# Raw keys and a transfer in place of two TensorE transposes in a pipelined delta rule

## The chip, the cores and the metric

The kernel runs on one core of a Trainium2 chip. The metric is device time in microseconds (us) for one execution of the whole program.

## The reference

A decoder layer on x of shape (4, 512, 512): a gated delta rule attention, a retention-like cross attention, and a ternary feed-forward net, each after a layer norm and added to x. The change touches the first alone:

```python
mixed = jax.nn.silu(_causal_conv1d(hidden_states @ w_qkv, conv_w))
q, k, v = jnp.split(mixed, [KDIM, 2 * KDIM], axis=-1)
q = _l2norm(q.reshape(Bb, Ss, HK, DK))          # x * rsqrt(sum(x*x) + eps), per token and head
k = _l2norm(k.reshape(Bb, Ss, HK, DK))
...
def step(St, inp):                               # over 512 tokens, per head
    q_t, k_t, v_t, g_t, b_t = inp
    St = St * jnp.exp(g_t)[..., None, None]
    v_old = jnp.einsum('bhk,bhkv->bhv', k_t, St)
    delta = (v_t - v_old) * b_t[..., None]
    St = St + k_t[..., None] * delta[:, :, None, :]
    return St, jnp.einsum('bhk,bhkv->bhv', q_t, St)
```

There are 16 key heads (HK), 32 value heads (two per key head), and head width 128. The output of each head is RMS-normed, gated with silu(z) and projected.

## The kernel before

`head` makes the normed input (xT, features on partitions) and tables of decays. `delta_rule` does the attention up to the output rows in DRAM (core_rows). `tail` does the rest. The change is inside `delta_rule`.

The work of `delta_rule` is cut into 64 units: 16 key heads times 4 batches (ITERS = 64). A unit holds one key head, its two value heads (GV = 2) and 512 tokens in four chunks of 128 (NC = 4). Within a chunk the step recurrence becomes a triangular system; its inverse is built in six levels. The units are software-pipelined. In slot u, unit n = u is projected (`project`), unit m = u - 1 is inverted (`invert`), unit s = u - 2 is run through the recurrence (`recur`), and unit f = u - 3 is finished (`finish`). TensorE, VectorE, ScalarE, GpSimd and the DMA queue (SyncE) each have a `slot` function in which this order is written out by hand. An engine runs its list in order and waits on semaphores, so a waiting instruction holds up all that stand behind it.

The steps and their lines on TensorE: `tile(n, j)` L722 projects a tile of k, q, v0 or v1 (j = 0, 1, 2, 3), `z_tile` L735 the gate; `turn` L742 is four transposes into a PSUM bank; `products` L747 is the four 128x128 products of `kk` and `kq`. `level_z` is L790 and `level_d` L803, eight small f16 products each, `level_e` L815. `solve` is L864, `read_q` L851, `read_k` L843, `grow` L872 and `attend` L883.

On VectorE: `convolve` L1007 is a tap of the causal convolution, `decays` L1016 a scan, `level_z` L1042, `level_d` L1046, `level_e` L1052, and `flip_d` L1035 the transpose of the inverse inside 32x32 blocks. `next_state` is L1072 and `residual` L1066. `flip_v` L1022 and `flip_o` L1027 turn values and outputs.

A level of the inverse goes back and forth between the two engines: TensorE `level_z(m, l)` waits for d_added of the level before; VectorE masks the result (`level_z`, z_ready); TensorE `level_d(m, l)` waits for z_ready and for `flip_d` of the level before (flipped); VectorE adds it (`level_d`, d_added).

The keys before the change: silu writes `kraw` (features on partitions). `k_turn` turns it into bank 2, so that tokens lie on partitions; ScalarE sums the squares, GpSimd makes the norm factor `rk` (L579, L582), and `normal_k` writes `khat`, the normed keys, token-major. `khat_turn` turns them back, ScalarE copies them to `kT`, and `kk` and `kq` multiply from kT. The queries stay raw; `q_turn` turns them for the sum of squares alone (`q_square`, L1195), which enters the RMS norm of the output.

All projections share three PSUM banks. RING_ORDER and RING_BANK say in which order and where; `ring_free` makes a step wait until the step that last had its bank is read. The waits of the ring for bank 1:

```python
RING_FREED = {... "v1": (taps, "taps", 11), ...}   # the last tap of v1, VectorE convolve(n, 3, 3)
```

Of the kernel before, what the change touches and what calls it, by code (L numbers as in the profile page):

```python
# [37 lines left out]
STORES = 16 * NC * NC  # L38

# [275 lines left out]
def delta_rule(nc, xT, tabs, cons, nw, wc, w_loaded, taps_loaded, acc, early_loaded, early_weighed, decay_dram, w_dram, v_dram, core_dram, wout):  # L315

    with ExitStack() as ctx:
# [22 lines left out]
        kss, qss, rkt, rk = sb("kss", [P, NC]), sb("qss", [P, NC]), sb("rkt", [P, NC]), sb("rk", [P, NC])  # L340
# [10 lines left out]
        tab_ready, decay_loaded, gam_ready, gamc_ready, gams_ready = sem("tab_ready"), sems("decay_loaded"), sem("gam_ready"), sem("gamc_ready"), sem("gams_ready")  # L351
        k_turned, k_squares, rk_ready = sem("k_turned"), sem("k_squares"), sem("rk_ready")
        khat_ready, khat_turned, kT_ready, ks_ready = sem("khat_ready"), sem("khat_turned"), sem("kT_ready"), sem("ks_ready")
        q_turned, q_squares, eq_ready = sem("q_turned"), sem("q_squares"), sem("eq_ready")
# [71 lines left out]
        def per_token(ap):  # L426
# [5 lines left out]
        RING_ORDER = ("q", "k", "z1", "v1", "k_turn", "z0", "kq", "v0", "khat_turn", "q_turn", "kk")  # L432
        RING_BANK = {"q": 1, "k": 2, "z1": 0, "v1": 1, "k_turn": 2, "z0": 0, "kq": 2, "v0": 0, "khat_turn": 2, "q_turn": 2, "kk": 1}
        RING_FREED = {"k": (taps, "taps", 2), "q": (taps, "taps", 5), "v0": (taps, "taps", 8), "v1": (taps, "taps", 11),
                      "z0": (z_silued, "z_silued", 0), "z1": (z_silued, "z_silued", 1),
                      "k_turn": (khat_ready, "squares", NC - 1), "khat_turn": (kT_ready, "once", 0), "q_turn": (q_squares, "squares", NC - 1),
                      "kk": (kk_copied, "once", 0), "kq": (kqs_ready, "once", 0)}
# [9 lines left out]
        RING_LAG = {"q": 1, "k": 0, "z1": 2, "v1": 0, "k_turn": 0, "z0": 2, "kq": 1, "v0": 0, "khat_turn": 0, "q_turn": 1, "kk": 0}  # L447
# [24 lines left out]
        def _(sp):  # L472
# [5 lines left out]
            def load_decay(n):  # L478
                g, b = n[0] * (ROUND // B) + n[1] // B, n[1] % B
                src = decay_dram[g, :, b, :] if isinstance(g, int) else decay_dram[bass.ds(g, 1), :, b, :].rearrange("a h s -> (a h) s")  # L480
                wait(sp, gam_ready, at(back(n, 2), GV, GV))
                sp.dma_start(decay[n[1] % 2][:, :, :], bc(src, P, 0)).then_inc(decay_loaded[n[1] % 2], 16)
# [3 lines left out]
            def slot(n, project, invert, recur, finish):  # L486
                if n[0] * ROUND + n[1] < ITERS - 1:
                    load_decay((n[0], n[1] + 1))
# [6 lines left out]
                if project:  # L495
                    next_weights(n, 3)
                if invert:
# [11 lines left out]
                if project:  # L509
                    next_weights(n, 2)  # L510

# [24 lines left out]
            def store_v(m):  # L536
                sp.wait_ge(v_flipped, count(m))
# [27 lines left out]
        def _(pool):  # L565
# [11 lines left out]
            def k_norm(n):  # L577
# [4 lines left out]
                nc.gpsimd.tensor_tensor(rk[:, :], rkt[:, :], cons[:, C_POW:C_POW + NC], ALU.pow).then_inc(rk_ready, 1)  # L582
# [35 lines left out]
            def b_full(n, h):  # L618
                pool.wait_ge(kk_copied, count(n))
# [4 lines left out]
            def p_full(m, h):  # L624
                pool.wait_ge(kqs_ready, count(m))
# [17 lines left out]
            def o_norm(s):  # L643
                pool.wait_ge(o_squares, at(s, GV * NC, GV * NC))
                nc.gpsimd.tensor_tensor(m2[:, :, :], oss[:, :, :], bc(eq[s[1] % 4][:, :], GV), ALU.add).then_inc(or_ready, 1)
# [17 lines left out]
            def slot(n, project, invert, recur, finish):  # L663
# [32 lines left out]
                if project:  # L696
                    gate_strict(n, 0)
                    b_full(n, 0)
# [5 lines left out]
                if invert:  # L704
                    q_norm(m)
                    decayed_keys(m, 1)

# [3 lines left out]
        def _(pe):  # L711
# [38 lines left out]
            def k_turn(n):  # L750
                pe.wait_ge(silued, nth(n, "silued", 0))
                ring_free(n, "k_turn")
                turn(bank("k_turn"), kraw, k_turned)

            def khat_turn(n):
                pe.wait_ge(khat_ready, at(n, NC, NC))
                ring_free(n, "khat_turn")
                turn(bank("khat_turn"), khat[n[1] % 2], khat_turned)

            def q_turn(n):  # L760
                pe.wait_ge(silued, nth(n, "silued", 1))
                ring_free(n, "q_turn")
                turn(bank("q_turn"), qT[third(n)], q_turned)

            def kk(n):
                pe.wait_ge(kT_ready, count(n))
                ring_free(n, "kk")
                products(bank("kk"), kT[third(n)], kT[third(n)], kk_done)

            def kq(m):  # L770
                pe.wait_ge(kT_ready, count(m))
                pe.wait_ge(silued, nth(m, "silued", 1))
                ring_free(m, "kq")
                products(bank("kq"), kT[third(m)], qT[third(m)], kq_done)
# [66 lines left out]
            def read_k(s, c):  # L841
                state_ready(s, c)
                nc.tensor.matmul(psa[:, 0:GV * P], chunk(kT[third(s)], c), state[:, :], start=True, stop=True).then_inc(ks_s, 1)  # L843
# [53 lines left out]
            def slot(n, project, invert, recur, finish):  # L897
# [82 lines left out]
                if invert:  # L980
                    level_z(m, 3)
                    q_turn(m)
# [3 lines left out]
                if project:  # L986
                    kk(n)
# [9 lines left out]
        def _(dve):  # L997
# [12 lines left out]
            def decays(n, h):  # L1010
# [3 lines left out]
                dve.wait_ge(decay_loaded[r % 2], q * (ROUND * 8) + (r // 2 * 16 + 16))  # L1014
                wait(dve, bf_ready, nth(n, "bf_ready", h, 1))
                nc.vector.tensor_tensor_scan(gam[h][:, :], decay[r % 2][:, h, :], ident[:, :], 0.0, ALU.mult, ALU.add).then_inc(gam_ready, 1)  # L1016

            def flip_v(m):
# [3 lines left out]
                nc.vector.transpose(vb[:, :, :, :], vraw[:, :, :].rearrange("p h (c b j) -> p b (h c) j", c=NC, b=NC)).then_inc(v_flipped, 1)  # L1022

# [57 lines left out]
            def slot(n, project, invert, recur, finish):  # L1081
# [81 lines left out]
                if invert:  # L1163
                    level_e(m, 4)
# [4 lines left out]
        def _(act):  # L1169
# [8 lines left out]
            def silu(n, j):  # L1178
                act.wait_ge(taps, nth(n, "taps", 3 * j + 2))
                if j == 0:  # L1180
                    wait(act, k_turned, count(n, 1))
                if j >= 2:
                    wait(act, v_flipped, count(n, 1))
                v = vraw
                out = (kraw[:, :], qT[third(n)][:, :], v[:, 0, :], v[:, 1, :])[j]
# [7 lines left out]
            def squares(src, spare, dst, sem_, scale=1.0):  # L1193
                for c in range(NC):
                    nc.scalar.activation(junk[:, spare + c, :], chunk(src, c), ACT.Square, scale=scale,  # L1195
                                         accum_out=dst[:, c:c + 1]).then_inc(sem_, 1)

            def k_square(n):
                act.wait_ge(k_turned, count(n))
                wait(act, rk_ready, at(back(n, 1), 2, 1))  # L1200
                wait(act, q_squares, at(back(n, 2), NC, NC))
                squares(bank("k_turn"), 0, kss, k_squares)

            def q_square(n):
                act.wait_ge(q_turned, count(n))
# [921 lines left out]
```

## Time and profile before

| | us |
|---|---|
| median of 3 runs | 3333.22 |
| lowest and highest | 3330.68, 3338.06 |
| the profiled execution | 3335.47 |
| its span | 3333.6 |
| its granted clock of TensorE, mean | 0.991 |

The median and the profiled execution are two different executions; a sum made on the trace is made against 3335.47. `delta_rule` fills about the first 2490 us of the span. A slot repeats there with the same pattern, so that one slot can be read for all. In the rows, L790 and so on are lines of the kernel before. Buffer numbers are left out of names: acc is any of the four PSUM banks of the ring and of td, d_conv either convolution buffer. A row of a timeline that says x8 holds eight instructions and their common duration; the start of the next row of the same engine says when that engine went on.

### The profile page before, as it was taken

What the parts mean: (1) busy time and instruction counts of PE and PEld (TensorE: products, weight loads), DVE (VectorE), ACT (ScalarE), POOL (GpSimd) and SP (SyncE); (2) the same over time, 40 slices, a digit from 0 to 9 for tenths busy, and PEclk for the clock granted to TensorE, in tenths of its full rate; (3) what the DMA queues carried; (4) which work ended last, traced back from release to release, by engine and by line L of the source; (5) the groups of instructions that cost most, each with busy time, mean ns of one, the idle gap of its engine ahead of it and who ended that gap; (6) DMA issues with size and microseconds to landing.
All of it is one profiled execution on the core that took longest, in us unless ns stands there. A gap on an engine that the chain in (4) does not pass through costs nothing. (4 is left out here: it accounts for less than half of the span.)

```text
span 3333.6 us, 59535 instructions
## 1 busy us (share of the span) xinstructions
PE 3238.8 (97%) x20832; PEld 2152.7 (65%) x20832; DVE 2414.8 (72%) x3622; ACT 1541.4 (46%) x4983; POOL 1863.5 (56%) x1824
## 2 busy tenths in 40 slices
PE   5899999999999999999999999999988999999999
PEld 2577777777777777777777777777764444454444
DVE  6799999999999999999999999999940011034453
ACT  2455556555655555556555655565631000011232
POOL 2677777777777777777777777777740000011132
PEclk8999999999999999999999999999989999999999
DMA  2122322323232323322332233223215222211001
GB/s 101 42 61 77 70 71 58 77 64 71 64 77 64 71 65 71 73 65 61 78 71 69 58 78 67 67 66 77 75 52 211 76 101 101 76 38 64 0 13 38
DMA packets 373958, 231.85 MB, mean 70 GB/s; under 512 B 290304, under 2 KB 323200, under 8 KB 368128
## 3 DMA queue, kind: packets, MB, share of 16 engines
q1 hardware_dynamic: 372368, 220.97, 25.4%
q10 hardware_dynamic: 1296, 7.08, 0.5%
q8 instruction: 170, 2.79, 0.4%
q14 instruction: 124, 1.02, 0.1%
HBM read 156.39 MB, written 71.57 MB: 68 GB/s over the span
## 5 line engine op out<-in xcount | busy, mean ns | idle before, releaser
L722 PE MATMUL acc<-xT,wc 128*128 128x512 f32 x2048 | 935.8, 600 | 2.8 <-PEq L111 2.0
L722 PEld LDWEIGHTS acc<-xT,wc 128*128 128x128 f32 x2048 | 370.2, 191 | 373.2 <-issue 372.5
L1007 DVE SCALAR_TENSOR_TENSOR d_conv<-acc,wc,d_conv 128x511 f32<-128x511 f32 (+2 forms) x768 | 567.0, 738 | 42.7 <-ACT d_conv L1176 33.5
L735 PE MATMUL acc<-wc,xT 128*128 128x256 f32 x2048 | 473.4, 384 | 0.0
L735 PEld LDWEIGHTS acc<-wc,xT 128*128 128x128 f32 x2048 | 379.1, 190 | 46.2
L622 POOL TENSOR_TENSOR d_bf<-d_kks,d_gam 128x512 f32<-128x512 f32 x128 | 160.3, 1273 | 317.9 <-ACT d_kks L1222 317.9
L1530 PE MATMUL acc<-t_area 128*128 128x512 f32 x768 | 332.5, 592 | 1.0 <-ACT t_area L1979 1.0
L1035 DVE STREAM_TRANSPOSE d_em<-d_dm 128x1024 f16<-128x1024 f16 x256 | 314.5, 1229 | 2.2
L2036 POOL TENSOR_SCALAR t_veps<-t_mv 128x1 f32<-128x1 f32 x32 | 9.7, 303 | 546.1 <-DVE t_mv L1775 546.1
L1042 DVE TENSOR_TENSOR d_zm<-d_tz,cons 128x512 f16<-128x512 f32 x384 | 259.1, 675 | 52.7 <-PE d_tz L790 47.7
L1765 DVE TENSOR_TENSOR t_x<-acc,t_x 128x512 f32<-128x512 f32 x16 | 11.1, 692 | 392.4 <-PE acc L1530 392.4
L1176 ACT ACTIVATE d_conv<-acc,wc 128x512 f32<-128x512 f32 x256 | 175.0, 683 | 183.2 <-PE acc L722 107.5
L1530 PEld LDWEIGHTS acc<-t_area 128*128 128x128 f32 x768 | 144.6, 190 | 177.4 <-issue 177.1
L656 POOL TENSOR_TENSOR d_oo<-d_oo,d_sz 128x512 f32<-128x512 f32 x128 | 159.9, 1269 | 162.5 <-ACT d_oo L1228 162.5
L1016 DVE TENSOR_TENSOR_SCAN d_gam<-d_decay,d_ident 128x512 f32<-128x512 f32 x128 | 247.2, 1931 | 1.4 <-DMA d_decay<-decay_rows 1.4
L640 POOL TENSOR_TENSOR d_imd<-cons,d_dm 128x512 f16<-128x512 f32 x128 | 211.7, 1654 | 59.9 <-ACT d_dm L1245 59.9
L1046 DVE TENSOR_TENSOR d_dm<-acc,d_dm 128x512 f16<-128x512 f32 x256 | 175.6, 686 | 49.2 <-PE acc L803 49.2
L1927 ACT ACTIVATE xT<-t_turn 128x512 f32<-128x512 f32 x32 | 18.2, 596 | 369.7 <-PE t_turn L1512 369.7
L790 PEld LDWEIGHTS d_tz<-d_dm,d_bh 128*128 128x128 f16 x3072 | 136.9, 98 | 75.2 <-issue 39.5
L803 PEld LDWEIGHTS acc<-d_zm,d_em 128*128 128x128 f16 x3072 | 138.5, 98 | 61.9 <-issue 37.9
L883 PE MATMUL d_psb<-d_uu,d_pT 128*128 128x128 f32 x1024 | 161.2, 280 | 7.1 <-ACT d_oq L1249 7.1
L1258 ACT ACTIVATE d_uu<-d_psa 128x256 f32<-128x256 f32 x256 | 99.6, 389 | 141.0 <-PE d_psa L864 137.8
(227 smaller groups left out, 7084.5 us busy)
## 6 DMA issues: line engine op xcount, KB each, us to landing
d_decay<-decay_rows SPq DMA_DIRECT2D x64, 512.0 KB, 5.2
v_rows<-d_vb SPq DMA_DIRECT2D x256, 128.0 KB, 2.3
d_vn<-v_rows SPq DMA_DIRECT2D x64, 512.0 KB, 3.6
core_rows<-d_ob SPq DMA_DIRECT2D x1024, 32.0 KB, 1.7
t_area<-core_rows SPq DMA_DIRECT2D x30, 1024.0 KB, 4.8
wc<-in_w SPq DMA_DIRECT2D x96, 256.0 KB, 3.3
t_x<-in_x SPq DMA_DIRECT2D x4, 1024.0 KB, 9.6
t_area<-in_wout ACTq DMA_DIRECT2D x2, 2048.0 KB, 13.4
```

Source lines behind the costliest of these rows:

```text
L622: nc.gpsimd.tensor_tensor(bf[h][:, :], kks[:, :], gam[h][:, :], ALU.mult).then_inc(bf_ready, 1)
L640: nc.gpsimd.tensor_tensor(half_of(imd, 5)[:, :, 0, :], bc(cons[:, C_ID + (1 - side) * HALF:C_ID + (2 - side) * HALF], GV * NC), half_of(dm ...
L722: last = nc.tensor.matmul(bank(TILE[j])[:, :], wtile(j, k), xT[:, k, r % B * S:(r % B + 1) * S], start=k == 0, stop=k == KT - 1)
L735: last = nc.tensor.matmul(bank(f"z{j}")[:, i * GV * P:(i + 1) * GV * P].rearrange("p (h n) -> p h n", h=GV), xT[:, k, r % B * S + (2 * j + ...
L883: last = nc.tensor.matmul(chunk(psb, h), chunk(pT[s[1] % 2][h], c), chunk(uu, h), start=True, stop=True)
L1007: nc.vector.scalar_tensor_tensor(c[:, d:S], bank(TILE[j])[:, 0:S - d], tap(j, KS - 1 - d), c[:, d:S], ALU.mult, ALU.add).then_inc(taps, 1)
L1016: nc.vector.tensor_tensor_scan(gam[h][:, :], decay[r % 2][:, h, :], ident[:, :], 0.0, ALU.mult, ALU.add).then_inc(gam_ready, 1)
L1035: nc.vector.transpose(em[m[1] % 2][:, :], dm[:, :]).then_inc(flipped, 1)
L1042: nc.vector.tensor_tensor(even(zm[l], l), packed(tz, l), bc(mask, GV * NC), ALU.mult).then_inc(z_ready, 1)
L1046: nc.vector.tensor_tensor(even(dm, l), packed(td, l), even(dm, l), ALU.add).then_inc(d_added, 1)
L1176: nc.scalar.activation(conv_of(TILE[j])[:, :], bank(TILE[j])[:, :], ACT.Copy, scale=tap(j, KS - 1)).then_inc(tap0, 1)
L1530: return nc.tensor.matmul(acc[t][:, :], core_of(grp, t, q, h), rhs, start=head == 0, stop=head == HV - 1)
```

## The change

Keys stay raw. silu writes straight into `kT` (four buffers now), and `kk`, `kq` and `read_k` use raw keys. The key norm enters as a factor per row: the ScalarE copies of kk and kq go chunk by chunk with scale `rk`, and the factor of the residual is a new table `rt` (`state_scale` on GpSimd). kk needs the norm per column too: rk is stored to DRAM and loaded back to all partitions as `krow` (`store_row`, `load_row`), and GpSimd multiplies (`column_scale`). So `khat_turn` and `copy_kT` go. `q_turn` goes as well: VectorE turns the queries in 32x32 blocks (`flip_q`), 16 transfers move the blocks (`move_q`), and `q_square` reads the result a slot later. `copy_kq` is cut into four scaled pieces in the same way as `copy_kk` below. The two buffers of `decay` become one. On TensorE `kk` is placed elsewhere.

```diff
-        RING_ORDER = ("q", "k", "z1", "v1", "k_turn", "z0", "kq", "v0", "khat_turn", "q_turn", "kk")
+        RING_ORDER = ("q", "k", "z1", "v1", "k_turn", "z0", "kq", "kk", "v0")
...
-                wait(sp, gam_ready, at(back(n, 2), GV, GV))
+                wait(sp, gam_ready, at(back(n, 1), GV, GV))
             def slot(n, project, invert, recur, finish):
+                if invert:
+                    next_weights(back(n, 1), 1)
+                if project:
+                    next_weights(n, 0)
+                if invert:
+                    next_weights(back(n, 1), TILES)
+                if project:
+                    next_weights(n, 3)
                 if n[0] * ROUND + n[1] < ITERS - 1:
                     load_decay((n[0], n[1] + 1))
...
+                if project:
+                    store_row(n)
                 if invert:
                     store_v(back(n, 1))
+                if project:
+                    load_row(n)
...
+                if invert:
+                    move_q(back(n, 1))
...
+            def store_row(n):
+                sp.wait_ge(rk_ready, at(n, 2, 2))
+                sp.dma_start(row_dram[n[1] % 2], rk[n[1] % 4][:, :]).then_inc(row_moved, 16)
+            def load_row(n):
+                sp.wait_ge(row_moved, at(n, 32, 16))
+                wait(sp, kk_ready, count(n, 1))
+                sp.dma_start(krow[:, :], bc(row_dram[n[1] % 2].rearrange("p c -> (p c)"), P, 0)).then_inc(row_moved, 16)
+            def move_q(m):
+                sp.wait_ge(v_flipped, at(m, 2, 2))
+                wait(sp, q_squares, at(back(m, 1), NC, NC))
+                for a in range(NC):
+                    for b in range(NC):
+                        sp.dma_start(qn[b * 32:(b + 1) * 32, a].rearrange("p c j -> p (c j)"),
+                                     qf[a * 32:(a + 1) * 32, b].rearrange("p c j -> p (c j)")).then_inc(q_moved, 16)
...
+            def state_scale(n):
+                pool.wait_ge(tab_ready, count(n))
+                pool.wait_ge(rk_ready, at(n, 2, 2))
+                nc.gpsimd.tensor_tensor(rt[n[1] % 4][:, :].rearrange("p (h c) -> p h c", h=GV),
+                                        tab(n, Q_NEGDEC).rearrange("p (h c) -> p h c", h=GV), bc(rk[n[1] % 4][:, :], GV),
+                                        ALU.mult).then_inc(rt_ready, 1)
+            def column_scale(n):
+                pool.wait_ge(kk_copied, at(n, NC, NC))
+                pool.wait_ge(row_moved, at(n, 32, 32))
+                nc.gpsimd.tensor_tensor(by_chunk(kks), by_chunk(kks), krow[:, :].rearrange("p (i c) -> p c i", c=NC), ALU.mult).then_inc(kk_ready, 1)
                     k_norm(n)
+                    state_scale(n)
...
                     gate_strict(n, 0)
+                    column_scale(n)
                     b_full(n, 0)
...
             def kk(n):
-                pe.wait_ge(kT_ready, count(n))
+                pe.wait_ge(silued, nth(n, "silued", 0))
                 ring_free(n, "kk")
...
                     kq(m)
                     level_z(m, 2)
                 if project:
+                    kk(n)
                     tile(n, 2)
                 if invert:
                     level_d(m, 2)
-                if project:
-                    khat_turn(n)
...
                     level_z(m, 3)
-                    q_turn(m)
                 if recur:
                     grow(s, 1)
-                if project:
-                    kk(n)
                 if invert:
                     level_d(m, 3)
...
+            def flip_q(m):
+                dve.wait_ge(silued, nth(m, "silued", 1))
+                wait(dve, q_moved, at(back(m, 1), MOVED, MOVED))
+                nc.vector.transpose(qf[:, :, :, :], qT[third(m)][:, :].rearrange("p (c b j) -> p b c j", c=NC, b=NC)).then_inc(v_flipped, 1)
...
                 if invert:
+                    flip_q(m)
                     level_e(m, 4)
...
             def copy_kk(n):
+                act.wait_ge(rk_ready, at(n, 2, 2))
-                nc.scalar.activation(kks[:, :], bank("kk")[:, :], ACT.Copy).then_inc(kk_copied, 1)
+                for c in range(NC):
+                    nc.scalar.activation(chunk(kks, c), chunk(bank("kk"), c), ACT.Copy, scale=rk[n[1] % 4][:, c:c + 1]).then_inc(kk_copied, 1)
...
                     copy_kq(m)
+                if project:
+                    copy_kk(n)
                 if recur:
                     first_output(s)
-                if project:
-                    copy_kT(n)
...
-                if invert:
-                    q_square(m)
                 if recur:
+                    q_square(s)
                     solved(s, 2)
```

TensorE in the middle of a slot, before. d_qT,d_kT is `kq`, the L722 row is the tile v0, d_khat is `khat_turn`:

```order
L747 MATMUL acc<-d_qT,d_kT 128x128 x4
L790 MATMUL d_tz<-d_dm,d_bh_0 128x64 x4
L790 MATMUL d_tz<-d_dm,d_bh_1 128x64 x4
L722 MATMUL acc<-xT,wc 128x512 x4
L803 MATMUL acc<-d_zm,d_em 128x64 x8
L742 MATMUL acc<-cons,d_khat 128x128 x4
```

And the end of the same slot, before. d_qT is `q_turn`, d_kT alone is `kk`, the last row is `read_k(s, 2)`:

```order
L742 MATMUL acc<-cons,d_qT 128x128 x4
L872 MATMUL d_psa<-d_uu,d_ks_0 128x128
L872 MATMUL d_psa<-d_uu,d_ks_1 128x128
L747 MATMUL acc<-d_kT 128x128 x4
L803 MATMUL acc<-d_zm,d_em 128x64 x8
L843 MATMUL d_psa<-d_state,d_kT 128x256
```

TensorE of the changed kernel, the first of these places. L789 is `products`, L822 `level_z`, L764 `tile`, L835 `level_d`, L896 `solve`:

```order
L789 MATMUL acc<-d_qT,d_kT 128x128 x4
L822 MATMUL d_tz<-d_dm,d_bh_0 128x64 x4
L822 MATMUL d_tz<-d_dm,d_bh_1 128x64 x4
L789 MATMUL acc<-d_kT 128x128 x4
L764 MATMUL acc<-xT,wc 128x512 x4
L835 MATMUL acc<-d_zm,d_em 128x64 x8
L896 MATMUL d_psa<-d_rr,d_tt_0 128x128
```

`kk` stands ahead of tile v0 and of `level_d(m, 2)` now; both transposes are gone, and between `level_d(m, 2)` and `level_d(m, 3)` only `solve`, `read_q`, `level_z` and `grow` are left.

VectorE at the end of a slot of the changed kernel. L1075 is `level_z(m, 4)`, L1068 `flip_d`, L1035 the three taps of v0, L1085 `level_e`:

```order
L1075 TENSOR_TENSOR d_zm<-d_tz,cons 128x16x32
L1068 STREAM_TRANSPOSE d_em<-d_dm 128x1024
L1035 SCALAR_TENSOR_TENSOR d_conv<-acc,wc,d_conv 128x511
L1035 SCALAR_TENSOR_TENSOR d_conv<-acc,wc,d_conv 128x510
L1035 SCALAR_TENSOR_TENSOR d_conv<-acc,wc,d_conv 128x509
L1055 STREAM_TRANSPOSE d_qf<-d_qT 128x512
L1085 TENSOR_TENSOR d_em<-d_te,d_em 128x16x32
```

The row d_qf<-d_qT is new; before, `level_e` stood right behind the taps. The rest of VectorE's list is as it was.

## Rows read from the trace of the kernel before

**Rows 1.** One slot: length, busy PE, PEld, DVE, ACT, POOL; clock, DMA share, GB/s
```profile
1300.41:1337.22 36.81, 36.81 (x286) 27.14 (x285) 34.09 (x51) 21.77 (x75) 27.21 (x27) 1.00 0.26 56
```

**Rows 2.** Timeline of TensorE, end of a slot: start, duration, engine, line, operation
```profile
1295.59 0.40 PE L803 MATMUL acc<-d_zm,d_em 128*128 128x64 f16 x8
...
1297.41 0.63 PE L742 MATMUL acc<-cons,d_qT 128*128 128x128 f32 x4
1297.88 0.61 PE L872 MATMUL d_psa<-d_uu,d_ks 128*128 128x128 f32 x4
1298.33 1.06 PE L747 MATMUL acc<-d_kT 128*128 128x128 f32 x8
1299.22 0.40 PE L803 MATMUL acc<-d_zm,d_em 128*128 128x64 f16 x8
1299.45 0.68 PE L843 MATMUL d_psa<-d_state,d_kT 128*128 128x256 f32 x2
1299.97 0.61 PE L883 MATMUL d_psb<-d_uu,d_pT 128*128 128x128 f32 x4
1300.41 0.40 PE L790 MATMUL d_tz<-d_dm,d_bh 128*128 128x64 f16 x8
```

**Rows 3.** Timeline of VectorE, same stretch; in brackets its idle time and who ended it
```profile
1296.03 0.69 DVE L1046 TENSOR_TENSOR d_dm<-acc,d_dm 128x512 f16<-128x512 f32 x1 [0.18 <-PE acc L803]
1296.75 1.25 DVE L1035 STREAM_TRANSPOSE d_em<-d_dm 128x1024 f16<-128x1024 f16 x1
1297.92 0.65 DVE L1042 TENSOR_TENSOR d_zm<-d_tz,cons 128x512 f16<-128x512 f32 x1
1298.53 0.61 DVE L1072 SCALAR_TENSOR_TENSOR d_state<-d_state,d_tabm,d_psa 128x128 f32<-128x128 f32 x2
1299.65 0.69 DVE L1046 TENSOR_TENSOR d_dm<-acc,d_dm 128x512 f16<-128x512 f32 x1 [0.52 <-PE acc L803]
...
1302.87 2.27 DVE L1007 SCALAR_TENSOR_TENSOR d_conv<-acc,wc,d_conv 128x511 f32<-128x511 f32 x3
1305.71 0.69 DVE L1052 TENSOR_TENSOR d_em<-d_te,d_em 128x512 f16<-128x512 f32 x1 [0.57 <-PE d_te L815]
```

**Rows 4.** Timeline of all engines around `level_z(m, 2)`, one slot later
```profile
1328.10 0.74 DVE L1007 SCALAR_TENSOR_TENSOR d_conv<-acc,wc,d_conv 128x509 f32<-128x509 f32 x1
...
1328.66 0.40 PE L790 MATMUL d_tz<-d_dm,d_bh 128*128 128x64 f16 x8
```

**Rows 5.** Timeline near the end of the delta rule, where TensorE waits for VectorE
```profile
2458.72 0.68 DVE L1062 TENSOR_TENSOR d_tt<-d_te,d_em 128x512 f32<-128x512 f32 x1
...
2459.46 0.38 PE L864 MATMUL d_psa<-d_vn,d_tt 128*128 128x128 f32 x1 [0.22 <-DVE d_tt L1062]
```

**Rows 6.** Groups by line and shape, 1000 to 2000 us: busy us, mean ns | idle
```profile
L1022 DVE STREAM_TRANSPOSE d_vb<-d_vraw 128x1024 f32<-128x1024 f32 x27 | 33.3, 1234 | 0.0
L1235 ACT ACTIVATE d_khat<-acc,d_rk 128x128 f32<-128x128 f32 x108 | 30.8, 368 | 8.4 <-issue 8.4
```

**Rows 7.** Timeline of GpSimd: the norm factor rk, and the first product with kks
```profile
1300.09 2.51 POOL L622 TENSOR_TENSOR d_bf<-d_kks,d_gam 128x512 f32<-128x512 f32 x2 [4.79 <-ACT d_kks L1222]
...
1322.93 1.01 POOL L582 TENSOR_TENSOR d_rk<-d_rkt,cons 128x4 f32<-128x4 f32 x1
...
1330.85 1.27 POOL L593 TENSOR_TENSOR d_gam<-d_gamc,cons 128x512 f32<-128x512 f32 x1
```

**Rows 8.** DMA issues of the page: KB each, median us from issue to landing
```profile
v_rows<-d_vb SPq DMA_DIRECT2D x256, 128.0 KB, 2.3
...
wc<-in_w SPq DMA_DIRECT2D x96, 256.0 KB, 3.3
```

**Rows 9.** Timeline of the DMA queue: issue of one unit's 16 output stores
```profile
1295.38 9.51 SPq L555 DMA_DIRECT2D core_rows<-d_ob  x16
```

**Rows 10.** Busy time in two stretches with TensorE waits (columns as in Rows 1)
```profile
2436.99:2446.08 9.09, 6.58 (x45) 5.68 (x45) 5.72 (x10) 2.53 (x12) 2.60 (x4) 0.62 0.51 141
2446.00:2460.00 14.00, 11.13 (x117) 9.20 (x115) 8.57 (x17) 5.33 (x20) 8.77 (x6) 1.00 0.06 10
```

More of the change, by code:

```diff
@@ L446, in delta_rule @@
                     "zr_ready": (1, 2), "closed": (2, 1), "tt_ready": (2, 1)}
-        RING_LAG = {"q": 1, "k": 0, "z1": 2, "v1": 0, "k_turn": 0, "z0": 2, "kq": 1, "v0": 0, "khat_turn": 0, "q_turn": 1, "kk": 0}
+        RING_LAG = {"q": 1, "k": 0, "z1": 2, "v1": 0, "k_turn": 0, "z0": 2, "kq": 1, "v0": 0, "kk": 0}
         CONV_LAG = {"k": 0, "v1": 0, "v0": 0, "q": 0}
@@ L752, in k_turn @@
                 ring_free(n, "k_turn")
[L753 to L763, printed above, removed]
+                turn(bank("k_turn"), kT[n[1] % 4], k_turned)
             def kk(n):
-                pe.wait_ge(kT_ready, count(n))
+                pe.wait_ge(silued, nth(n, "silued", 0))
                 ring_free(n, "kk")
-                products(bank("kk"), kT[third(n)], kT[third(n)], kk_done)
+                products(bank("kk"), kT[n[1] % 4], kT[n[1] % 4], kk_done)
             def kq(m):
-                pe.wait_ge(kT_ready, count(m))
+                pe.wait_ge(silued, nth(m, "silued", 0))
                 pe.wait_ge(silued, nth(m, "silued", 1))
                 ring_free(m, "kq")
-                products(bank("kq"), kT[third(m)], qT[third(m)], kq_done)
+                products(bank("kq"), kT[m[1] % 4], qT[third(m)], kq_done)
             def piece(t, h, c):
@@ L842, in read_k @@
                 state_ready(s, c)
-                nc.tensor.matmul(psa[:, 0:GV * P], chunk(kT[third(s)], c), state[:, :], start=True, stop=True).then_inc(ks_s, 1)
+                nc.tensor.matmul(psa[:, 0:GV * P], chunk(kT[s[1] % 4], c), state[:, :], start=True, stop=True).then_inc(ks_s, 1)
             def read_q(s, c):
@@ L1180, in silu @@
                 if j == 0:
-                    wait(act, k_turned, count(n, 1))
+                    wait(act, ks_s, at(back(n, 4), 3, 3))
                 if j >= 2:
-                    wait(act, v_flipped, count(n, 1))
+                    wait(act, v_flipped, at(back(n, 1), 2, 1))
                 v = vraw
-                out = (kraw[:, :], qT[third(n)][:, :], v[:, 0, :], v[:, 1, :])[j]
+                out = (kT[n[1] % 4][:, :], qT[third(n)][:, :], v[:, 0, :], v[:, 1, :])[j]
                 nc.scalar.activation(out, conv_of(TILE[j])[:, :], ACT.Silu).then_inc(silued, 1)
@@ L1200, in k_square @@
                 wait(act, rk_ready, at(back(n, 1), 2, 1))
-                wait(act, q_squares, at(back(n, 2), NC, NC))
-                squares(bank("k_turn"), 0, kss, k_squares)
+                wait(act, k_squares, at(back(n, 1), NC, NC))
+                squares(lambda c: chunk(bank("k_turn"), c), lambda c: junk[:, c, :], kss, k_squares)
             def q_square(n):
-                act.wait_ge(q_turned, count(n))
+                act.wait_ge(q_moved, at(n, MOVED, MOVED))
                 wait(act, eq_ready, count(n, 1))
-                wait(act, k_squares, min(at(back(n, -1), NC, NC), NC * ITERS))
-                squares(bank("q_turn"), 0, qss, q_squares, scale=(RMS_EPS * HD) ** 0.5)
-            def copy_kT(n):
-                act.wait_ge(khat_turned, count(n))
-                nc.scalar.activation(kT[third(n)][:, :], bank("khat_turn")[:, :], ACT.Copy).then_inc(kT_ready, 1)
+                squares(lambda c: qn[:, :, c, :], lambda c: qn[:, :, c, :], qss, q_squares, scale=(RMS_EPS * HD) ** 0.5)
             def b_high(n, h):
@@ L1234, in normal_k @@
                 for c in range(NC):
[L1235 removed]
+                    nc.scalar.activation(chunk(khat[n[1] % 2], c), chunk(bank("k_turn"), c), ACT.Copy, scale=rk[n[1] % 4][:, c:c + 1]).then_inc(khat_ready, 1)
             def copy_kq(m):
@@ L1239, in copy_kq @@
                 wait(act, p_ready, at(back(m, 1), GV, GV))
-                nc.scalar.activation(kqs[:, :], bank("kq")[:, :], ACT.Copy).then_inc(kqs_ready, 1)
+                for c in range(NC):
+                    nc.scalar.activation(chunk(kqs, c), chunk(bank("kq"), c), ACT.Copy, scale=rk[m[1] % 4][:, c:c + 1]).then_inc(kqs_ready, 1)
             def copy_d(m, l, n):
```

60 lines of the change are left out of this document (32 added, 28 removed).

## The prediction

> **What bounds the kernel now.** I read the windows first. In one whole slot, from one `level_z(m, 4)` of TensorE to the next, TensorE is busy 36.81 of 36.81 us, VectorE 34.09, GpSimd 27.21, ScalarE 21.77, and the clock is granted in full, 1.00 [rows 1]. A busy TensorE proves little, since ends of matmuls are modelled, so I went to its timeline: each step starts where the one before it lets it, and no row has a wait in brackets [rows 2]. VectorE's rows do have such brackets: it waits 0.18, 0.52 and 0.57 us for TensorE [rows 3]. So TensorE sets the slot, and VectorE is 36.81 - 34.09 = 2.72 us from doing so. The question is not only how much TensorE loses in work, but whether VectorE can hand back each level of the inverse in time once TensorE comes sooner. I look at the end of the slot, where the edits lie.
>
> **What TensorE saves.** `q_turn` runs from 1297.41 to the start of `grow` at 1297.88, 0.47 us [rows 2]. `khat_turn` is four transposes of the same shape and gets the same 0.47. Together 0.94 us per slot. `kk` is not removed but moved, with 1299.22 - 1298.33 = 0.89 us [rows 2]. Slots with projection and recurrence together are u = 2 to 63, 62 of them. If nothing waited, the gain would be 62 x 0.94 = 58 us.
>
> **What stands in its way.** Before, the stretch from `level_d(m, 2)` at 1295.59 to `level_z(m, 4)` at 1300.41 takes 4.82 us on TensorE [rows 2], and all of it is work. Both turns and `kk` lie in it. All three leave it, so TensorE has 4.82 - 0.94 - 0.89 = 2.99 us of work left there. The chain through VectorE is longer. Let t be the start of `level_d(m, 2)` on TensorE (1295.59 before). From rows 3:
> VectorE `level_d` starts at t + 0.44 (1296.03), `flip_d` at t + 1.16, `level_z(m, 3)` at t + 2.33 and ends 0.65 later at t + 2.98; the two `next_state` start at t + 2.94 and end 0.61 later at t + 3.55.
> A TensorE step that really waits for VectorE starts 0.06 us after it ends: the VectorE operation ends at 2458.72 + 0.68 = 2459.40, TensorE starts at 2459.46 [rows 5].
> So TensorE `level_d(m, 3)`, which needs z_ready, starts at t + 3.04. It would have been ready after d2, solve, read_q, level_z and grow, well under t + 2. `read_k(s, 2)` needs the new state: t + 3.55 + 0.06 = t + 3.61. Behind it `attend` starts 0.52 later and `level_z(m, 4)` 0.44 after that [rows 2], at t + 4.57. (The other way to it, through VectorE's add of level 3, gives t + 3.55 + 0.69 + 0.06 = t + 4.30, which is earlier.) The stretch shrinks from 4.82 to 4.57, by 0.25 us and not by 1.83, and TensorE idles 4.57 - 2.99 = 1.58 us in it.
>
> **What `kk` costs in its new place.** It stands between `level_z(m, 2)` and tile v0, where TensorE has no slack, so t itself comes 0.89 us later. It needs bank 1 back from v1, whose last tap ends at 1328.10 + 0.74 = 1328.84, so 1328.90 with the handoff. TensorE would get there at 1328.66 + 0.23 (the spacing 1299.22 to 1299.45 of such a group) = 1328.89 [rows 2, 4]. So 0.01 us, nothing.
>
> **Per slot:** + 0.89 + 0.01 - 0.25 = + 0.65 us, a slot of 37.46. Before, `kk` filled time in which VectorE was at work on the chain; now it stands ahead of the chain, and the transposes that go were filling the same time.
>
> **The edits that cost nothing as I read them, and what covers them.**
> `flip_q`, VectorE: 128x512 elements, half of `flip_v`, whose mean is 1.234 us [rows 6]; half is 0.62. It stands between the last tap of v0 and `level_e`. There VectorE waits 0.57 us for TensorE: taps from 1302.87, 2.27 long, then `level_e` at 1305.71 [rows 3]. By the chain above VectorE's `level_z(m, 4)` follows TensorE's no later than before, so the wait absorbs it to 0.05 us. Bounds: 0, and 0.62 us per slot if the cover is gone.
> ScalarE: a copy becomes four pieces of 0.368 mean [rows 6], at most 1.47 each for kk and kq, less `copy_kT`. ScalarE has 15 us free in a slot [rows 1], and kk comes 1335.14 - 1328.90 = 6.2 us earlier than it did (1298.33 + 36.81 = 1335.14), so its copy ends earlier as well. `q_square` reads queries moved a slot before.
> GpSimd: `column_scale` is a 128x512 product like the neighbours of 1.27 us, with a strided operand. It can start once `gate_strict` ends at 1330.85 + 1.27 = 1332.12. Before, GpSimd stood idle 4.79 us for kks and began `b_full` at 1300.09, that is 1336.90 a slot later [rows 7]. Now it begins about 1333.4. `state_scale` works on 128x8 elements, far less than any of these, and GpSimd is free 9.6 us of a slot [rows 1].
> The row: rk is ready at 1322.93 + 1.01 = 1323.94 [rows 7]. SyncE needs 9.51 / 16 = 0.59 us per issue [rows 9]; `store_row` and the four `store_v` take five of them, to 1326.9. `store_row` lands in 2.3 by the nearest row, before that. `load_row` lands 3.3 us after it is issued, as a load of 256 KB does [rows 8], at 1330.2. `column_scale` cannot start before 1332.12, and `b_full` is where it was if the row lands by 1335.6. Between 2 and 5 us of cover.
> SyncE: `move_q` adds 16 issues, 9.5 us, to 9.5 for the stores and some 8 others: about 24 us of a 37 us slot. It is ahead of the next slot's decay load; that load's single buffer is free once `decays(n, 0)` has run in the first half of a slot and is read at the start of the next.
> Filling and draining slots (0, 1, 64 to 66) already have TensorE waiting; I take 0 for them, within 2 us.
>
> **The sum.** 62 x 0.65 = 40 us. The profiled execution took 3335.5 and would take 3375.8. The median of the runs is 2.25 lower, so the same sum gives 3333.2 + 40.3 = 3373.5. I forecast 3374, slower. Bounds of this case: with handoffs of 0 instead of two of 0.06, 0.53 per slot, 3366; with `flip_q` in full on the path, 1.27 per slot, 3412. I stay at the low end because the wait that covers `flip_q` stands in a row.
>
> **Rivals.**
> *The gain arrives in full* (faster). If VectorE's chain were not binding, each slot would lose 0.94 us: 3333 - 58 = 3275. It decides where the stretch from `level_d(m, 2)` to `level_z(m, 4)` can be run in less than 4.82 - 0.89 = 3.93 us. For it: TensorE waits nowhere before, and many brackets of VectorE are waits for TensorE. Against it: rows 3 hold 3.55 us of VectorE work and fixed lag alone, ahead of `read_k`. 12 in 100. Somewhere between the two, at no change, 8 in 100.
> *VectorE becomes the bound.* A slot of 36.81 + 0.62 = 37.43, 3372: nearly my time by another cause. The Trainium skill, page "Perfetto Trace Analysis", section "Identifying the Most-Contended Engine", holds that matmul busy time misleads and that TensorE should be judged by the busy share of its weight loads, the other engines by occupancy. By that rule VectorE is the most contended engine here (34.09 against 27.14 us of weight loads [rows 1]), removed transposes bring nothing, and the added one counts in full, which gives that 3372. Against it: VectorE's own waits name TensorE. What tells it apart is VectorE's idle time, which would go to zero. 5 in 100.
> *The row is late.* Beyond 1335.6 each further us is a us per slot, 62 us in all; with one, 3436. 5 in 100.
> *The clock falls.* Before, a stretch with 2.51 us of TensorE idle in 9.09 ran at a granted 0.62, partly at 1.2 GHz, while one with 2.87 idle in 14.00 kept 1.00 [rows 10]. Mine has 1.58 idle in 37.46, all within 4.57. Such a fall would cost 6.58 x 0.38 = 2.5 us per slot: 3374 + 155 = 3529. 4 in 100. The Trainium skill, page "TensorE: Matmul & The Clock Gate", part 1, says that the gate lets half the pulses through unless TensorE has lately been busy; the first of these two stretches agrees.
>
> **How the numbers follow.** My forecast has 66 in 100. A measurement of this kernel tells about 0.2%, 6.7 us, from no change. Slower takes the forecast, VectorE, the row and the clock: 80. Faster 12, same 8. The range takes in no change at its lower end and the full `flip_q` at its upper, 3328 to 3415; it leaves out the full gain, the clock and most of the late row. The forecast's own range is 3366 to 3412.
>
> **What the profile would show.** Right: a slot of about 37.5 us; TensorE waits of 1.6 us per slot, ended by VectorE's `level_z` ahead of `level_d(m, 3)` and by `next_state` ahead of `read_k(s, 2)`; VectorE waiting about 0.9 us more ahead of `level_d(m, 2)`; `flip_q` where 0.57 us of waiting was; no turns beside `k_turn`. Wrong: no such waits and a slot of 35.9 (the full gain); VectorE without idle time; GpSimd waiting for a DMA ahead of `column_scale`; a granted clock under 1.0. Most likely to break the forecast is a chain through VectorE shorter than I add it up, since 0.65 is a difference of larger numbers.

## The result, and the profile after

The changed kernel takes 3516.39 us (median of 4 runs, 3515.33 to 3518.67), the kernel before 3331.95 beside it: a ratio of 1.055, 95% interval 1.053 to 1.057. The direction was forecast, the size was not: 3374 with a range of 3328 to 3415. The span grew from 3333.6 to 3513.5 us, by 179.9.

The start of `flip_o` on VectorE (the row d_ob<-d_oo) comes once a slot, so its spacing is the length of a slot. I took it for 60 slots of each kernel; every fourth of them begins a new key head.

| mean slot, us | before | after |
|---|---|---|
| 45 slots within a key head | 36.81 | 37.50 |
| 15 slots with a new key head | 37.47 | 47.23 |
| sum of the 60 | 2218.7 | 2396.0 |

Of the 177.3 us in these slots, 45 x 0.69 = 31 lie in the ordinary ones and 15 x 9.76 = 146 in the others. So two things have to be read, and they are in different places.

**An ordinary slot.** The timeline of TensorE of the changed kernel, at the stretch of [rows 2]; L835 is `level_d`, L822 `level_z`, L875 `read_k`, L915 `attend`:

```profile
1300.75 0.40 PE L822 MATMUL d_tz<-d_dm,d_bh 128*128 128x64 f16 x8
1301.08 1.13 PE L789 MATMUL acc<-d_kT 128*128 128x128 f32 x8
1302.05 3.60 PE L764 MATMUL acc<-xT,wc 128*128 128x512 f32 x8
1305.48 0.40 PE L835 MATMUL acc<-d_zm,d_em 128*128 128x64 f16 x8
...
1308.52 0.41 PE L835 MATMUL acc<-d_zm,d_em 128*128 128x64 f16 x8 [0.92 <-DVE d_zm L1075]
1309.03 0.70 PE L875 MATMUL d_psa<-d_state,d_kT 128*128 128x256 f32 x2
1309.56 0.61 PE L915 MATMUL d_psb<-d_uu,d_pT 128*128 128x128 f32 x4
1310.01 0.40 PE L822 MATMUL d_tz<-d_dm,d_bh 128*128 128x64 f16 x8
```

And VectorE in the same stretch; the row d_qf is `flip_q`:

```profile
1305.91 0.69 DVE L1079 TENSOR_TENSOR d_dm<-acc,d_dm 128x512 f16<-128x512 f32 x1 [1.15 <-PE acc L835]
1306.64 1.25 DVE L1068 STREAM_TRANSPOSE d_em<-d_dm 128x1024 f16<-128x1024 f16 x1
1307.81 0.65 DVE L1075 TENSOR_TENSOR d_zm<-d_tz,cons 128x512 f16<-128x512 f32 x1
1308.38 0.58 DVE L1106 SCALAR_TENSOR_TENSOR d_state<-d_state,d_tabm,d_psa 128x128 f32<-128x128 f32 x2
...
1314.57 0.70 DVE L1055 STREAM_TRANSPOSE d_qf<-d_qT 128x512 f32<-128x512 f32 x1
1315.30 0.69 DVE L1085 TENSOR_TENSOR d_em<-d_te,d_em 128x512 f16<-128x512 f32 x1
1315.91 1.22 DVE L1044 TENSOR_TENSOR_SCAN d_gam<-d_decay,d_ident 128x512 f32<-128x512 f32 x1
```

With t = 1305.48, `level_d(m, 3)` starts at t + 3.04 and `level_z(m, 4)` at t + 4.53. TensorE waits for VectorE's `level_z` (L1075) where before it had a turn and `kk` to do. VectorE's wait for `level_d(m, 2)` on TensorE has grown from 0.18 [rows 3] to 1.15, because `kk` now delays that step. `flip_q` is in the place of the old wait of 0.57. The whole ordinary slot, in the columns of [rows 1]:

```profile
1272.51:1310.01 37.50, 36.48 (x279) 26.41 (x277) 34.06 (x52) 22.30 (x80) 28.04 (x29) 1.00 0.36 83
```

**A slot with a new key head.** The next rows of the same timelines, in the slot that follows. TensorE:

```profile
1323.06 0.40 PE L847 MATMUL d_te<-d_em,d_zm 128*128 128x64 f16 x8
1330.35 1.19 PE L915 MATMUL d_psb<-d_uu,d_pT 128*128 128x128 f32 x4 [6.89 <-ACT d_oq L1281]
```

VectorE (the row of 1317.04 holds the last three taps of the old key head), and below it ScalarE, which both of them wait for (L1211 is `first_tap`):

```profile
1317.04 2.29 DVE L1035 SCALAR_TENSOR_TENSOR d_conv<-acc,wc,d_conv 128x511 f32<-128x511 f32 x3
...
1329.14 0.75 DVE L1035 SCALAR_TENSOR_TENSOR d_conv<-acc,wc,d_conv 128x511 f32<-128x511 f32 x1 [8.70 <-ACT d_conv L1211]
```

```profile
1328.42 0.69 ACT L1211 ACTIVATE d_conv<-acc,wc 128x512 f32<-128x512 f32 x1 [11.22 <-DMA wc<-in_w]
1329.01 0.36 ACT L1281 ACTIVATE d_oq<-d_psb,d_tabm 128x128 f32<-128x128 f32 x1
```

The DMA queue (SyncE), a row giving the start of the first issue of its kind and the time that all of them took:

```profile
1304.30 9.07 SPq L581 DMA_DIRECT2D core_rows<-d_ob  x16
1313.41 0.45 SPq L479 DMA_DIRECT2D wc<-in_w  x1
1315.30 10.02 SPq L572 DMA_DIRECT2D d_qn<-d_qf  x16
1325.36 1.06 SPq L479 DMA_DIRECT2D wc<-in_w  x2
```

Read from below: the last two loads are the q weights and the convolution taps of the new key head, in this order. The taps have one buffer, so their load waits for the last tap of the old key head, which ends at 1317.04 + 2.29 = 1319.33. But until 1325.3 the queue is busy with the 16 issues of `move_q`, and the load goes out more than 6 us late. ScalarE stands at the first tap 11.22 us. Behind it in ScalarE's list is `read_q` (L1281), so its result for `attend` is late, and TensorE stands 6.89 us. Before, ScalarE's wait for the taps was there too, but shorter. The waits over 100 to 2500 us of the kernel before, the row for these loads:

```profile
ACT d_conv L1176 <- DMA wc<-in_w: 72.2, 15, 5.3
```

and after, over the same window:

```profile
ACT d_conv L1211 <- DMA wc<-in_w: 174.2, 15, 12.7
```

That is 4.8 us at each new key head before, and 11.6 after. TensorE's waits for `read_q` behind that tap, in the same two answers, before and then after:

```profile
PE d_psb L883 <- ACT d_oq L1249: 7.1, 15, 1.0
```

```profile
PE d_psb L915 <- ACT d_oq L1281: 109.2, 15, 8.3
```

So TensorE already waited 0.5 us at each new key head before the change, and waits 7.3 now. It pays once more behind its wait. In windows of the changed kernel (columns as in [rows 1]), 1323.06 to 1338.09 holds the wait and what follows it, 1330.35 to 1338.09 only what follows it, and 1375.82 to 1385.53 is ordinary work:

```profile
1323.06:1338.09 15.03, 8.14 (x44) 5.32 (x41) 7.23 (x12) 4.70 (x15) 7.19 (x6) 0.77 0.31 59
1330.35:1338.09 7.74, 7.74 (x30) 5.01 (x31) 6.02 (x10) 2.80 (x8) 7.19 (x6) 0.68 0.42 70
1375.82:1385.53 9.71, 9.71 (x99) 8.96 (x97) 8.68 (x13) 8.10 (x34) 5.51 (x8) 1.00 0.47 92
```

The granted clock is 0.77 on the mean of the first and 0.68 on that of the second: `attend` takes 1.19 us where it takes 0.61 at 1309.56. From `attend` to the end of tile v1 TensorE needs 7.74 us. The kernel before has the same steps in one of its ordinary slots:

```profile
1313.70:1319.05 5.35, 5.35 (x37) 3.20 (x34) 5.35 (x9) 2.78 (x8) 4.88 (x5) 1.00 0.01 2
```

TensorE is busy throughout in both windows, so the 2.39 us between them are put down to the clock. This slot is 46.94 us long (its `flip_o` starts at 1303.03, the next at 1349.97), 9.44 more than an ordinary one: 6.89 of waiting and 2.39 of slow clock make 9.28 of it.

### The profile page after: what moved, and what is told of

Read it like the earlier page. It is cut to its first block and busy times, and to the rows that moved or that the text cites. A ratio compares the mean times of both kernels' runs of the same rounds, so it can differ in the third digit from the quotient of the medians.

```text
span 3513.5 us, 60809 instructions
## 1 busy us (share of the span) xinstructions
PE 3251.3 (93%) x20320; PEld 2134.0 (61%) x20320; DVE 2414.0 (69%) x3686; ACT 1577.3 (45%) x5303; POOL 1923.5 (55%) x1952
## 3 DMA queue, kind: packets, MB, share of 16 engines
q8 instruction: 166, 2.72, 0.3%
## 5 line engine op out<-in xcount | busy, mean ns | idle before, releaser
L764 PE MATMUL acc<-xT,wc 128*128 128x512 f32 x2048 | 944.0, 604 | 2.1 <-PEq L112 2.0
L1035 DVE SCALAR_TENSOR_TENSOR d_conv<-acc,wc,d_conv 128x511 f32<-128x511 f32 (+2 forms) x768 | 567.4, 739 | 155.9 <-ACT d_conv L1211 146.6
L764 PEld LDWEIGHTS acc<-xT,wc 128*128 128x128 f32 x2048 | 376.7, 194 | 380.8 <-issue 379.8
L678 POOL TENSOR_TENSOR d_imd<-cons,d_dm 128x512 f16<-128x512 f32 x128 | 160.9, 1257 | 384.1 <-ACT d_dm L1277 384.1
L1211 ACT ACTIVATE d_conv<-acc,wc 128x512 f32<-128x512 f32 x256 | 175.6, 686 | 353.0 <-PE acc L764 178.7
L1068 DVE STREAM_TRANSPOSE d_em<-d_dm 128x1024 f16<-128x1024 f16 x256 | 314.7, 1229 | 2.2
L1075 DVE TENSOR_TENSOR d_zm<-d_tz,cons 128x512 f16<-128x512 f32 x384 | 259.9, 677 | 64.5 <-PE d_tz L822 58.0
L915 PE MATMUL d_psb<-d_uu,d_pT 128*128 128x128 f32 x1024 | 169.0, 290 | 109.2 <-ACT d_oq L1281 109.2
L915 PEld LDWEIGHTS d_psb<-d_uu,d_pT 128*128 128x128 f32 x1024 | 146.2, 200 | 115.7 <-issue 112.3
L835 PEld LDWEIGHTS acc<-d_zm,d_em 128*128 128x128 f16 x3072 | 133.2, 98 | 131.6 <-DVE d_zm L1075 74.6
L835 PE MATMUL acc<-d_zm,d_em 128*128 128x64 f16 x3072 | 154.0, 193 | 63.5 <-DVE d_zm L1075 62.4
L1044 DVE TENSOR_TENSOR_SCAN d_gam<-d_decay,d_ident 128x512 f32<-128x512 f32 x128 | 196.8, 1538 | 1.6 <-DMA d_decay<-decay_rows 1.6
L822 PEld LDWEIGHTS d_tz<-d_dm,d_bh 128*128 128x128 f16 x3072 | 138.1, 98 | 77.4 <-issue 36.7
```

Source lines behind the costliest of these rows:

```text
L678: nc.gpsimd.tensor_tensor(half_of(imd, 5)[:, :, 0, :], bc(cons[:, C_ID + (1 - side) * HALF:C_ID + (2 - side) * HALF], GV * NC), half_of(dm ...
L764: last = nc.tensor.matmul(bank(TILE[j])[:, :], wtile(j, k), xT[:, k, r % B * S:(r % B + 1) * S], start=k == 0, stop=k == KT - 1)
L835: last = nc.tensor.matmul(packed(td, l, (h * NC + c) * HALF, HALF), piece(em[m[1] % 2], h, c), even(zm[l], l, (h * NC + c) * P, P), start= ...
L915: last = nc.tensor.matmul(chunk(psb, h), chunk(pT[s[1] % 2][h], c), chunk(uu, h), start=True, stop=True)
L1035: nc.vector.scalar_tensor_tensor(c[:, d:S], bank(TILE[j])[:, 0:S - d], tap(j, KS - 1 - d), c[:, d:S], ALU.mult, ALU.add).then_inc(taps, 1)
L1044: nc.vector.tensor_tensor_scan(gam[h][:, :], decay[:, h, :], ident[:, :], 0.0, ALU.mult, ALU.add).then_inc(gam_ready, 1)
```

## The experiments

All ratios are against the kernel before, run beside the experiment. Slots are given as mean of the 45 ordinary ones / mean of the 15 with a new key head.

**1. Moves later.** The changed kernel, with the moves behind the loads of weights and taps:

```diff
                 if invert:
                     next_weights(back(n, 1), TILES)
+                if recur:
+                    move_q(back(n, 2))
...
-                if invert:
-                    move_q(back(n, 1))
```

> The changed kernel, with the 16 moves of the queries issued in the next slot, behind the loads of the q and k weights and of the taps instead of ahead of them. Theory A (order on the queue): the 15 slots with a new key head, 47.3 us each in the changed kernel, wait because 10.0 us of issues stand ahead of the tap load; they fall to 37.5 to 38.5, and the kernel takes 3516 - 15 x 9.3 = about 3377 us. Theory B (traffic: the moves themselves slow the other transfers, or the clock falls for the steady idle time): the moves are still there, the long slots stay above 44 us, and the time stays above 3460.

3370.87 us, ratio 1.012 (1.010 to 1.013); slots 37.50 / 37.50. Theory A. The transfers are all still there, so neither their traffic nor the steady idle time of TensorE made the long slots. The result is also near the 3374 of the prediction, in part by luck, as the section on the prediction says.

**2. kk back.** On top of experiment 1 (its place in RING_ORDER and its copy on ScalarE go back with it):

```diff
                 if project:
-                    kk(n)
                     tile(n, 2)
...
                     grow(s, 1)
                     head_start(s, 4)
+                if project:
+                    kk(n)
```

> As the kernel with the moves later, and kk back in its old place, between grow and level_d(m, 3), with its copy where it was. Chain theory: kk then fills time in which TensorE waits for VectorE anyway; a slot falls from 37.50 by 0.94 to 36.56, and the kernel by 62 x 0.94 = 58 us against the moves later, to about 3319. Rival (the place of kk is free, and something else lengthens the slot): no change against the moves later, about 3377. Third way: GpSimd gets kks later by the copy in pieces and by column_scale, and part of the gain goes there, 3325 to 3350.

3361.15 us, ratio 1.009 (1.007 to 1.010); slots 37.33 / 37.32. This fits none of the three numbers that were written down: it gained 0.18 us per slot, not 0.94. The third way named the right engine, but took too little of the gain away. The waits between 1000 and 2000 us have a row that was not there before:

```profile
DVE d_zr L1091 <- POOL d_imd L678: 32.4, 26, 1.5
```

VectorE waits 1.2 us per slot for GpSimd's `i_minus_d`. Experiment 9 takes that up.

**3. Keys alone.** The changed kernel without `flip_q` and `move_q`; the queries are turned on TensorE again:

```diff
                     level_z(m, 3)
+                    q_turn(m)
...
-                    flip_q(m)
-                if invert:
-                    move_q(back(n, 1))
```

> The changed kernel with the queries as before: q_turn on TensorE and q_square in the same slot, no flip_q, no moves. Raw keys, the row transfer and the one decay buffer stay. Theory A: slots with a new key head are normal again, about 37.5 to 38.5; the others stay at 37.50, since q_turn fills idle time (2.99 + 0.47 = 3.46 of work in a chain of 4.57). About 3375 us. Rival (the row transfer or the decay load ahead of others causes the long slots): they stay above 44, time above 3460.

3372.53 us, ratio 1.012 (1.011 to 1.014); slots 37.50 / 37.61. Theory A again. Against experiment 1 TensorE has 0.47 us more to do in the stretch, and the ordinary slot is 37.50 in both: work in that gap is free, so removing it brought nothing.

**4. Queries alone.** The kernel before with `flip_q`, `move_q`, no `q_turn`, and the one decay buffer with its place in the queue; keys as before.

> The kernel before with the query part of the change and the one decay buffer: flip_q, moves, no q_turn; keys as before, with khat_turn and kk in its old place. Theory A: the 15 slots with a new key head take about 47; the others have 4.82 - 0.47 = 4.35 us of TensorE work in the stretch and a chain of 4.57, so 36.56. 3333 - 62 x 0.25 + 15 x 9.5 = about 3460 us. Rival (the row transfer makes the long slots): none are long, about 3318.

3449.36 us, ratio 1.035 (1.034 to 1.037); slots 36.52 / 46.37. The long slots come with the moves, and raw keys and the row transfer are not needed for them. The ordinary slot is 0.29 shorter than before: with `kk` in its old place the chain takes over from 4.82 of work. In this run's own timeline `level_d(m, 2)` starts at 1319.72 and `level_z(m, 4)` at 1324.25, 4.53 later.

**5 and 6. Extra issues on the kernel before.** One decay buffer and the new order of loads, and copies of zeros at the end of the slot, 16 of them in experiment 5, 8 in experiment 6:

```diff
                 if project:
                     next_weights(n, 2)
+                if invert:
+                    extra_moves(back(n, 1))
```

> The kernel before with one decay buffer, the new order of the loads on the queue, and 16 extra copies of 16 KB within SBUF per slot, issued at the end of the slot where the changed kernel moves the queries. They carry zeros that nobody reads. No other part of the change. Theory A (issues ahead of the tap load): each of the 15 slots with a new key head gets about 9 us longer, the others stay at 36.81; 3333 + 15 x 9 = about 3468 us. Rival (the loss needs something of the query path, such as q_square waiting for the moves): no change, about 3325 to 3333.

> The same with 8 extra copies per slot instead of 16. Theory A: the queue is occupied 5.0 us instead of 10.0, and the slots with a new key head get about 4.5 us longer; about 3400 us. Rival (a threshold, or a fall of the clock that comes once the wait is there at all): the loss stays near that of 16 copies, or vanishes.

With 16: 3449.18 us, ratio 1.035 (1.033 to 1.036); slots 36.81 / 45.08. With 8: 3344.70 us, ratio 1.003 (1.002 to 1.004); slots 36.81 / 38.18. Experiment 7, which has neither, has 37.43 for the second number. So 16 issues that do nothing for the computation bring 7.65 us per new key head, most of the loss, where about 9 were expected. The dose was wrong: half the issues cost 0.75 us per new key head and not 4.5, which is nearer to the rival's threshold. The waits for the tap load, 100 to 2500 us, first with 16 and then with 8 (both are the same row of ScalarE as above):

```profile
ACT d_conv L1190 <- DMA wc<-in_w: 155.0, 15, 10.8
```

```profile
ACT d_conv L1190 <- DMA wc<-in_w: 82.6, 15, 6.6
```

10.3 and 5.5 us each, against 4.8 before. The queue shows why. In the kernel before, the two loads (q weights and taps) stand at their own waits, and below them is the VectorE row with the last three taps of the old key head:

```profile
1083.44 5.47 SPq L476 DMA_DIRECT2D wc<-in_w  x2
```

```profile
1086.26 2.28 DVE L1007 SCALAR_TENSOR_TENSOR d_conv<-acc,wc,d_conv 128x511 f32<-128x511 f32 x3
```

The two loads take 5.47 us where the changed kernel needs 1.06: the queue stands 4.4 us, until the old weights and taps have been used, the taps last at 1088.54. The same place with 8 issues and with 16:

```profile
1087.15 4.96 SPq L558 DMA_DIRECT2D d_qn<-d_qf  x8
1092.15 1.13 SPq L478 DMA_DIRECT2D wc<-in_w  x2
```

```profile
1125.57 10.02 SPq L558 DMA_DIRECT2D d_qn<-d_qf  x16
1135.63 1.05 SPq L478 DMA_DIRECT2D wc<-in_w  x2
```

Eight issues fill the time in which the queue stood anyway; with them the old taps are read at 1092.93 and the loads have gone by 1093.28. Sixteen outrun it: the old taps are read at 1131.29 and the loads go by 1136.68.

**7. One decay buffer and the order of the loads alone.**

> The kernel before with one decay buffer and the new order of the loads on the queue alone (weights and taps ahead of the decay row). If the one buffer costs a wait, slots get longer than 36.81. If the new order brings the taps sooner, the 15 slots of 37.4 with a new key head fall towards 36.81: 3333 - 15 x 0.6 = 3324 us.

3331.05 us, ratio 0.9996 (0.999 to 1.0005); slots 36.81 / 37.43. The single buffer is free, and so is the new order. The new order does not shorten the slots with a new key head, which I had thought possible.

**8. Queries alone, moves later.** Experiment 4 with the edit of experiment 1.

> The query part alone (keys as before, kk in its old place), with the moves behind the loads of weights and taps. Slots of 36.52 without long ones: 3333 - 62 x 0.29 - 15 x 0.6 = about 3306 us, faster than both kernels. Rival (the moves collide with something else in their new place when the keys take the old path, such as the value stores): slots above 36.81.

3312.48 us, ratio 0.994 (0.993 to 0.995); slots 36.52 / 37.14. This computes the reference and is faster than both kernels, by 0.6% against the kernel before. The slots with a new key head kept their 0.6 us, so it gained 20 us and not the expected 27.

**9. kk back, without the column factor.** Experiment 2 with `column_scale` on one element per partition; the column factor of the key norms is left out of kk:

```diff
-                nc.gpsimd.tensor_tensor(by_chunk(kks), by_chunk(kks), krow[:, :].rearrange("p (i c) -> p c i", c=NC), ALU.mult).then_inc(kk_ready, 1)
+                nc.gpsimd.tensor_tensor(kks[:, 0:1], kks[:, 0:1], krow[:, 0:1], ALU.mult).then_inc(kk_ready, 1)
```

> The kernel with moves later and kk back (37.32 us per slot), with column_scale cut to one element per partition: the column factor of the keys is left out of kk, its waits stay. Theory: kk back gained 0.18 and not 0.94 us per slot because column_scale, 1.54 us between the copy of kk and b_full on GpSimd, made GpSimd late for i_minus_d, for which VectorE waits 1.2 us per slot. Without it that wait goes, and the slot falls to 36.5 to 36.6: 3361 - 62 x 0.75 = about 3315 us. Rival (the copy of kk in four pieces on ScalarE, or the chain through VectorE itself, holds the slot): no change, or less than 0.3 us per slot, above 3343.

3304.02 us, ratio 0.991 (0.989 to 0.993); slots 36.52 / 36.71. The wait of VectorE for `i_minus_d` is down to 7.4 us in 21 times between 1000 and 2000 us. So `column_scale` is what kept experiment 2 from its gain. In the kernel before, GpSimd stood idle 4.79 us, but ahead of kks [rows 7]; `column_scale` comes behind kks, where experiment 2 shows VectorE waiting for it. Here the factor by columns was hidden only with kk computed early (experiment 1), and kk early costs TensorE 0.89 us.

## Why the prediction was right in one place and wrong in another

**The bound and the chain: right.** The prediction has an ordinary slot of 37.46; it is 37.50. It puts `level_d(m, 3)` at t + 3.04, `read_k` at t + 3.61, `level_z(m, 4)` at t + 4.57; the rows give 3.04, 3.55 and 4.53. Experiment 3 shows that work in the gap is free, experiment 9, with `kk` back and little on GpSimd, is 37.50 - 36.52 = 0.98 us below experiment 1; the prediction has `kk` ahead of the chain at 0.90. `kk` came a little later than foreseen: it starts 0.33 after `level_z(m, 2)`, not 0.24. Of the waits that were foretold on TensorE, the trace brackets 0.92 us ahead of `level_d(m, 3)`; the 1.5 are the chain of 4.53 less 2.99 of work.

**`flip_q`, the row, the single buffer: right as read.** `flip_q` took 0.70 us and not 0.62, inside VectorE's old wait. GpSimd waits 2.0 us in all for the row between 1000 and 2000 us of experiment 1. Experiment 7 puts the buffer at nothing.

**The queue: wrong, and this is the step that failed.** The prediction puts the cost of the 16 issues at nothing. It says of `move_q` that it "adds 16 issues, 9.5 us", that SyncE is busy "about 24 us of a 37 us slot", and that it is "ahead of the next slot's decay load". It stops there. Behind the moves also stand the q weights and the taps of the next key head, with ScalarE waiting for the taps 4.8 us already and with no slack: these slots were 37.47 and not 36.81. The issues made that wait 11.6 us and these slots 47.23. I had a mean slot and a sum of busy time, and a wait that comes once in four slots is in neither. The row of waits that names it (72.2 us in 15 times) was in the trace of before. The experiments show it three ways: move the issues (1 and 8), remove them (3), add empty ones (5), and each time the long slots go or come with them. It cost 146 of 180 us.

**The sum for ordinary slots: 31 us, not 40.** It counted 62 slots at 0.65. The 15 with a new key head were at 37.47 already, and experiment 1 has them at 37.50, so only the other 45 grew. That experiment 1 still lands at 3371 is partly luck: its span is 36.0 us longer than before, 31 of it in the 60 slots and 5.3 ahead of the first `flip_o` (at 189.43, before at 184.10), where the prediction took 0 within 2 us.

**The clock: right to be a rival, wrong in its place.** The steady idle time, 1.5 us per slot, left the clock alone (1.00 in the ordinary slot above; experiment 1: a mean of 0.99, as before). It fell behind waits of 7 us, and added 2.4 us in the slot that was read. The sum of that rival, 3529, comes near the result by accident: it had every slot slow.

**VectorE as the bound: did not happen.** It is idle 37.50 - 34.06 = 3.44 us of an ordinary slot, and was idle 2.72 before. In experiment 4, where TensorE lost 0.47 us of work and `kk` stayed in its place, the slot fell to 36.52.

**What stays open.** The 16 empty issues make slots of 45.08, the real moves of 46.37 and 47.23. Part of the first difference is in the waits for the tap load, 10.3 us with the empty issues and 11.8 in experiment 4: `move_q` itself waits for `flip_q` and starts later. The difference between the last two contains a chain that is also longer; it was not taken apart. The 0.6 us of the old slots with a new key head are for the most part the 0.5 us in which TensorE waits for `read_q`. That row is in experiments 7 and 8 as well (6.4 and 6.5 us in 15 times) and gone in 1 and 2; why the tap comes in time there was not shown.

## What to carry to other kernels

Where work is removed from an engine that never waits, add up the chain through the other engines over the same stretch: the slot cannot become shorter than the chain, and a step moved out of the stretch to a place without idle time is paid in full. When a transfer is added to a queue, list everything that is issued behind it in every kind of slot, also in those that come once in four, and look in the waits for the few that name a DMA: a wait of 5 us that costs almost nothing is a sign that the slack is used up. Several small issues in a row are one long one: here 16 of them take 10 us, with queries and with zeros alike.

## What the runs showed of the hardware

VectorE's scan (two inputs in SBUF) takes 1.22 us when GpSimd is idle as it starts and about 2.0 to 2.1 when GpSimd is at work. In the changed kernel GpSimd waits during one scan of each ordinary slot, and the mean of all scans falls. Groups of VectorE over 100 to 2500 us, before and then after:

```profile
L1016 DVE TENSOR_TENSOR_SCAN d_gam<-d_decay,d_ident 128x512 f32<-128x512 f32 x125 | 242.8, 1942 | 0.0
```

```profile
L1044 DVE TENSOR_TENSOR_SCAN d_gam<-d_decay,d_ident 128x512 f32<-128x512 f32 x120 | 184.6, 1538 | 0.0
```

It goes the other way too. In experiment 2 GpSimd starts a tiny product 0.14 us after a scan:

```profile
1320.48 1.26 DVE L1045 TENSOR_TENSOR_SCAN d_gam<-d_decay,d_ident 128x512 f32<-128x512 f32 x1
1320.62 1.12 POOL L654 TENSOR_TENSOR d_eq<-d_qss,cons 128x4 f32<-128x4 f32 x1
```

It lasts 1.12 us, to the end of the scan, where the same 128x4 product takes 0.20 in the kernel before. The Trainium skill, page "SBUF — State Buffer", section "Who interferes with whom", states that a VectorE instruction with two inputs in SBUF contends with a GpSimd instruction that reads SBUF; these rows agree. What this is worth in the time of the kernel was not measured.
